# Moving one third of the score reading, the last rounding and two moment blocks in the last twelve steps of a fused attention kernel

## The reference, cut to what matters

```
L   = einsum('bhqd,bhkd->bhqk', q, k) * scale            # 16 heads, head_dim 8, causal
L_y = einsum('bhqd,bhkd->bhqk', q, k_y) * scale
agg = sum(exp(clip(L_y, -15, 15)) * mask, -1) + EPS
r   = log(abs(L) + EPS) - log(agg + EPS)
w   = softplus(r) * mask
A   = w / (sum(w, -1) + EPS)
x   = x + (A @ v, heads joined) @ w_proj.T
x   = x + 0.5 * ffn(layernorm(x))                        # needs mean and variance of every row
```

## Time and profile before

| what | value |
|---|---|
| median of 3 runs | 408.61 us (408.25 to 410.2) |
| the profiled execution's own time | 409.16 us |
| its span in the profile | 407.3 us |
| busy in the span: PE, DVE, ACT, POOL | 326.3, 295.5, 289.1, 209.0 us |
| mean granted clock of PE | 0.872 of full speed |
| the last twelve steps | from about 275.3 to 326.6 us of the span |

### The profile page before, as it was taken

One profiled execution on the slowest core, in us unless ns is written; L12 is line 12 of the kernel. 1 busy time (PEld: TensorE's weight loads), 2 busy tenths in 40 slices (PEclk: granted clock), 3 DMA queues, 4 the chain that ended last, 5 costly groups with the idle time before them and its releaser, 6 DMA issues.

```text
span 407.3 us, 8267 instructions
## 1 busy us (share of the span) xinstructions
PE 326.3 (80%) x2412; PEld 194.3 (48%) x2412; DVE 295.5 (73%) x628; ACT 289.1 (71%) x686; POOL 209.0 (51%) x348
## 2 busy tenths in 40 slices
PE   6879999995776545778877688788878998899992
PEld 6639999642243211213323223242334454499992
DVE  5664443288879988999998989989998747644431
ACT  2915556324989999999998989995667658255561
POOL 6575645300335475677776766784540014765542
PEclk9989999996589955868968958888999899899997
DMA  8786755134478989003000030000300086577640
GB/s 250 262 239 187 215 167 164 45 105 137 130 203 219 227 206 211 0 2 85 22 1 2 0 105 1 2 0 3 103 2 2 0 253 214 170 210 209 167 133 28
DMA packets 37993, 47.61 MB, mean 117 GB/s; under 512 B 4288, under 2 KB 26816, under 8 KB 37696
## 3 DMA queue, kind: packets, MB, share of 16 engines
q1 hardware_dynamic: 33616, 36.20, 33.1%
q0 software_dynamic: 2560, 6.30, 5.3%
q10 hardware_dynamic: 1776, 4.60, 3.4%
HBM read 24.02 MB, written 6.29 MB: 74 GB/s over the span
## 4 chain that ended last, share of the span: by engine, by line
PE 42%; DVE 21%; ACT 15%; issue 7%; DMA 6%; POOL 4%; SPq 2%; ACTq 1%; POOLq 0%; DVEq 0%
PE PS L1673 11%; PE PS L1683 10%; PE PS L1829 6%; DVE R L1412 6%; ACT R L1039 4%; ACT R L1029 4%; ACT CL L1029 4%; DVE CL L1397 3%; PE PS L1807 3%; PE PS L1607 3%; DVE agg L1421 2%; DMA R<-rows_d,R 2%; SPq L507 2%; ACT R L1049 2%; PE PS L1792 2%
## 5 line engine op out<-in xcount | busy, mean ns | idle before, releaser
L1412 DVE TENSOR_TENSOR R<-PS,MB 128x1024 int32<-128x1024 int32 (+1 forms) x76 | 84.6, 1132 | 12.3 <-PE PS L1807 11.7
L1039 ACT ACTIVATE R<-R 128x1024 f32<-128x1024 f32 x64 | 78.6, 1273 | 9.3 <-DVE R L1412 9.3
L916 ACT ACTIVATE R<-PS,R 128x128 f32<-128x128 f32 x184 | 52.6, 368 | 40.7 <-PE PS L1673 40.7
L1792 PE MATMUL PS<-R 64*128 64x512 bf16 (+3 forms) x256 | 40.2, 368 | 29.1 <-DVE CL L1397 15.7
L1829 PE MATMUL PS<-R,V 128*32 128x256 f32 (+3 forms) x512 | 56.0, 540 | 4.0 <-ACT R L1039 4.0
L1807 PE MATMUL PS<-QPS,R 64*128 64x512 bf16 (+3 forms) x256 | 38.0, 347 | 22.7 <-DVE CL L1397 18.1
L1673 PE MATMUL PS<-R 128*128 (+1 forms) x368 | 51.2, 282 | 1.4 <-DVE R L1278 0.9
L1683 PE MATMUL PS<-R 128*128 (+1 forms) x368 | 48.8, 276 | 0.7 <-ACT R L916 0.7
L1673 PEld LDWEIGHTS PS<-R 128*128 128x128 f32 x368 | 44.6, 191 | 4.2 <-issue 1.5
L1683 PEld LDWEIGHTS PS<-R 128*128 128x128 f32 x368 | 44.7, 192 | 1.1 <-ACT R L916 1.1
L1397 DVE SCALAR_TENSOR_TENSOR CL<-PS,MA 128x1024 f32<-128x1024 f32 x32 | 38.9, 1215 | 6.8 <-PE PS L1792 6.4
(11 more groups left out here) (189 smaller groups left out, 554.4 us busy)
## 6 DMA issues: line engine op xcount, KB each, us to landing
R<-w SPq DMA_DIRECT2D x38, 258.0 KB, 3.6
R<-R SPq DMA_DIRECT2D x32, 128.0 KB, 2.4
R<-R SPq DMA_DIRECT2D x16, 256.0 KB, 6.3
QPS<-R SPq DMA_DIRECT2D x32, 128.0 KB, 2.4
R<-w ACTq DMA_DIRECT2D x8, 258.0 KB, 4.3
rows_d<-X SPq DMA_DIRECT2D x8, 256.0 KB, 4.2
R<-w ACTq DMA_DIRECT2D x1, 2048.0 KB, 8.8
rows_d<-R SPq DMA_DIRECT2D x8, 256.0 KB, 2.5
```

The costliest lines, as they stand in the source:

```text
L916: last = act.activation(HT[:, k % 2, c * P:(c + 1) * P], PS[:, k % 2, c * P:(c + 1) * P], ACT.Gelu, bias=W1[:, k, F + c:F + c + 1])
L1039: act.activation(w, w, ACT.Ln, bias=1.0, scale=1.0).then_inc(s_ln, 1)
L1412: dve.tensor_tensor(weights(v)[:, :, at:at + n].bitcast(i32), PS[:, SLOTS[slot(b_fill(v, g))], 0:n].bitcast(i32), spread(mask, 1, 2), ALU. ...
L1792: last = pe.matmul(PS[:, SLOTS[slot(n)], :][:, par, at:at + (i + 1) * P], QS[rows, hp, (b * TB + i) * P:(b * TB + i + 1) * P], YS[rows, hp ...
```

## The change

It has five parts.

1. `by_act(v, g)` is now g == 2 for every unit. ACT reads group 2 in steps 32 to 43 too, and POOL clears the triangle of twelve more units. PE's piece 3 waits for that triangle.
2. The turned heads go back into `AV_BANK`, beside the weighed output, for all units. So piece 0 of the next pair waits for `heads_out` on DVE and no longer only for `av_out` on ACT.
3. The rounding of the last batch's q in step 33 moves from DVE to ACT (`scaled_q(3)`).
4. `moments` of batch 0 moves from step 25 to step 36, and of batch 1 from step 32 to step 38.
5. Some products that only keep PE busy go to another bank.

```diff
+MOMENTS_AT = (STEPS + 4, STEPS + 6)
+ROUNDED = (1, 2, 3)
 def by_act(v, g):
-    return v + LAG < STEPS and g == 2
+    return g == 2
...
             for s in range(END_STEP):
-                if 0 < s - LAG <= STEPS - LAG:
+                if 0 < s - LAG <= STEPS:
                     lower_triangle(s - LAG - 1)
...
                     if 0 <= v < STEPS:
                         logs(v, 0)
+                        magnitudes(v)
+                    if s == (NB - 1) * HP + Q_AT:
+                        scaled_q(NB - 1)
...
-                if b not in MIDDLE:
+                if b not in ROUNDED:
                     dve.wait_ge(s_qt, b + 1)
-                    if b:
-                        dve.wait_ge(s_qps, STACK_DMAS * b)
                     dve.tensor_copy(QP3[:, 0, :], PS[:, 7, :]).then_inc(s_qhi, 1)
...
                     if b and at == X_AT:
                         residual(b)
+                        if b >= len(MOMENTS_AT):
+                            moments(b)
+                    if b < len(MOMENTS_AT) and s == MOMENTS_AT[b]:
                         moments(b)
...
-                if j == 2 and by_act(v, 2):
+                if j == 2:
                     pe.wait_ge(s_low, v + 2)
-                if piece == 0 and v and ao_shared(v - 2):
-                    pe.wait_ge(s_aot, v // 2)
-                elif piece == 0 and v:
+                if piece == 0 and v:
                     pe.wait_ge(s_ao, v)
...
             def weighed_t(v):
                 pe.wait_ge(s_aot, v // 2 + 1)
-                if ao_shared(v):
-                    slot_free(ao_fill(v + 3))
...
-                    idle_products(6)
+                    idle_products(6, RANK_BANKS[1][0])
```

More of the change, by code:

```diff
@@ L163, in slot @@
     return n % 2 if n < 3 * TWO_SLOTS else (n + 2) % 3
[L166 to L181, removed]
 def build(nc, x_in, wattn_in, wg_in, w1_in, w2_in, b2_in, out):
@@ L1035, in logs @@
                 act.wait_ge(s_read, dve_reads(b_fill(v, (0, 2)[part])))
-                if part == 1 and by_act(v, 2):
+                if part == 1:
                     act.wait_ge(s_mag, v + 1)
@@ L1428, in heads_out @@
                 w = 2 * (HD + 1)
-                bank = ao_bank(v)
                 for par in range(2):
@@ L1433, in heads_out @@
                         AO.rearrange("p i h c -> p i (h c)")[:, :, at:at + w],
-                        PS[:, bank, AO_COL:AO_COL + TB * 2 * w].rearrange("p (i r) -> p i r", i=TB)
+                        PS[:, AV_BANK, AO_COL:AO_COL + TB * 2 * w].rearrange("p (i r) -> p i r", i=TB)
                         [:, :, par * w:(par + 1) * w]).then_inc(s_ao, 1)
@@ L1543, in between @@
                         den_reciprocal(b)
[L1544 to L1548, removed]
+                    if b == 0 and at == X_AT + 1 and g == 0:
+                        residual(b)
             for s in range(END_STEP):
@@ L1561, in _ @@
                 for g in range(3):
-                    if 0 <= v < STEPS:
+                    if 0 <= v < STEPS and not by_act(v, g):
                         abs_scores(v, g)
@@ L1781, in slot_free @@
                         pe.wait_ge(s_read, dve_reads(before))
-                    if n - 3 in HEADS_IN:
-                        pe.wait_ge(s_ao, HEADS_IN[n - 3])
             def scores_a(s, g):
@@ L1842, in weighed_t @@
                     at = AO_COL + i * 4 * (HD + 1)
-                    last = pe.matmul(PS[:, ao_bank(v), at:at + 4 * (HD + 1)],
+                    last = pe.matmul(PS[:, AV_BANK, at:at + 4 * (HD + 1)],
                                      AOT[:, i * P:(i + 1) * P], used, start=True, stop=True)
@@ L1977, in _ @@
                     pe.wait_ge(s_read, dve_reads(fills_before(END_STEP) - 1))
+                    pe.wait_ge(s_mag, STEPS)
                     gate(1, 0, 0, 2)
@@ L1980, in _ @@
                     gate(1, 0, 2, 8)
-                    idle_products(6)
+                    idle_products(6, RANK_BANKS[1][0])
                 if s == LN_EARLY + 1:
-                    idle_products(3)
+                    idle_products(3, RANK_BANKS[1][0])
                 if s == LN_EARLY + 2:
```

## The result

The changed kernel takes 411.54 us (median of 20 runs, 408.95 to 412.9) where the kernel before, timed beside it, takes 408.44 (20 runs, 405.6 to 410.2). The ratio is 1.0068, interval 1.0048 to 1.0088: 2.8 us more. The quotient of the two medians is 1.0076, 3.1 us. The forecast was +2.6 us, 411.2. The profiled execution took 411.08 us, with a span of 409.3.

The account below looks back on a forecast made before the run. It took DVE to set the pace before the change and ACT after it. Its terms, -1.9 rounding, +4.6 queue, -1.7 up to step 44 and +1.6 clock, gave +2.6 us: 411.2 against 408.61, range 406.5 to 413.5.

Parts of the forecast that it names:

- DVE loses 6.6 us net, step 25 gives nothing back: Last twelve steps: small reads and rounding leave DVE, moments come in, net 6.6 us less; step 25 set at 0.
- The rounding ends 1.9 us earlier: Step 33: the rounding of q, now on ACT, ends at 284.56 instead of 286.48, a gain of 1.9 us.
- The POOL queue: Step 35: piece 3 of pair 20 waits 4.8 us for a triangle behind 6.46 us of POOL work; +4.6 net.
- Steps 36 to 44 win 1.7 back, 1.0 of it because a low stretch doesn't recur: Steps 36 to 44: lateness falls from 2.7 to 1.0 us, with about 1.0 won by running at full clock.
- ACT becomes the bound: Last twelve steps: ACT needs 6.2 us for two steps, its loop through PE 6.8, against DVE's 6.0 before.
- The clock costs 1.6: PE's clock falls in or behind the wait of step 35, costing 1.6 us.
- the two clock terms: About 1.0 us gained from the low stretch before step 44 not recurring, 1.6 lost to a fall at the wait.
- The rival for that case: The POOL queue doesn't matter: -1.9 at step 36, -1.7 behind it, -3.6 in all, 405.0 us; chance 0.14.
- the rival of x11: Low stretches kept off the wait come elsewhere: ratio stays 1.007, mean clock as with twelve products; no chance given.

Follow-up runs that it names:

- x4: The kernel before with only the moments moved (batch 0 from step 25 to 36, batch 1 from 32 to 38): ratio 1.0012 to the kernel before.
- x2: The changed kernel with POOL's triangle of unit 21 put ahead of `query_part` of batch 3: 406.04 us, ratio 0.9954 to the kernel before.
- x6: The changed kernel with eight more small operations on POOL ahead of the series of batch 3: 414.86 us, ratio 1.0159 to the kernel before.
- x5: The kernel before with only the rounding of the last batch's q moved to ACT: ratio 1.0012 to the kernel before.
- x1: The changed kernel with `query_part` of batch 3 spread over steps 35 to 39 on POOL: 404.73 us, ratio 0.9949 to the kernel before.
- x3: The changed kernel with twelve unused products keeping PE busy before piece 3 of pair 20: 410.53 us, ratio 1.0072 to the kernel before.
- x11: The changed kernel with 18 unused products in the wait before piece 3 of pair 20: ratio 1.0053 to the kernel before.
- x8: x1 with the moments of batches 0 and 1 in steps 42 and 43 instead of 36 and 38: ratio 0.9953 to the kernel before.
- x7: x1 with rounding and moments back in their old places: ratio 0.9972 to the kernel before.

## Why the prediction was right

Step by step, in its own order:

- **DVE loses 6.6 us net, step 25 gives nothing back.** Right. Between the same two instructions DVE's busy time fell from 46.3 to 40.1 us, by 6.3. x4 shows the exchange in step 25: 1.24 us of waiting for 1.19 of moments.
- **The rounding ends 1.9 us earlier.** Right. From the scores of unit 21 the end comes at 5.98 us (282.15 + 0.60 - 276.77), before at 7.11 (285.80 + 0.68 - 279.37): 1.1 earlier. But the changed kernel was at the lower clock there. In x2 and x6, whose clock was full, it comes at 5.14 (283.56 + 0.60 - 279.02) and 5.13 (285.75 + 0.60 - 281.22), so 2.0 earlier than before. The forecast had 5.2 (284.56 - 279.4) and 1.9. DVE waited 0.86 for it here and 1.0 in those two, where about 1 was forecast. The wait for the DMAs into `QPS` at step 36 is gone, as predicted. Alone (x5) the term is worth nothing that can be measured. ACT's rows of the rounding in x2 and in x6:

```profile
283.56 0.60 ACT L1053 ACTIVATE R<-PS 128x512 bf16<-128x512 f32 x1
```

```profile
285.75 0.60 ACT L1053 ACTIVATE R<-PS 128x512 bf16<-128x512 f32 x1
```

- **The POOL queue.** Right in mechanism and in size, and shown by removing it (x1, x2) and by making it longer (x6). Terms and series: 6.46 forecast, 6.44 measured. Piece 3 of pair 20 was to come 12.9 us after the scores of unit 21 (279.4 to 292.3) and came at 13.7 (276.77 to 290.50). In x6, whose clock was full there, it came at 297.72 - 281.22 = 16.5, less the added 3.6: 12.9. The wait was to be 4.8. It was 3.43, because PE itself arrived late at the lower clock; in x6 it is 8.41 - 3.6 = 4.8. At full clock step 36 would so be 2.8 late, where 2.7 was forecast: 12.9 to piece 3 and 4.24 from there to piece 0 of pair 22 (x3) make 17.1, against 293.73 - 279.37 = 14.4 before. This is an estimate from rows of three traces. The other triangles are hidden, as predicted: PE waits for POOL only this once. There are ten of them beside those of units 21 and 22, not twelve.
- **Steps 36 to 44 win 1.7 back, 1.0 of it because a low stretch doesn't recur.** The 1.0 was a mistake. From piece 0 of pair 22 to piece 1 of pair 30 the changed kernel needs 32.3 us at full clock, against a forecast of 32.0 and against 33.6 before with its low stretch. In this one trace the term came true, but x1 (311.34, 1.94 us for a piece that takes 1.06), x2, x3 (314.33) and x11 have a low stretch again and need 33.3 to 33.4, while x6 and x8 have none and need 32.3 and 32.2. x5, which keeps the order of the kernel before in these steps, happens to have none either and needs 33.26. The stretch belongs to an execution, not to the kernel. At full clock on both sides these steps win 1.0 (33.26 to 32.30), where 0.7 was forecast apart from the stretch. The windows of the kernel before and of x5:

```profile
293.73:327.38 33.65, 28.72 (x262) 12.56 (x261) 28.58 (x47) 24.80 (x25) 4.71 (x10) 0.95 0.04 11
```

```profile
290.03:323.29 33.26, 27.27 (x263) 12.45 (x261) 29.04 (x48) 24.81 (x25) 4.76 (x10) 1.00 0.04 9
```

- **ACT becomes the bound.** Right. ACT is busy 28.9 of 32.3 us behind step 36 and DVE, now with gaps, 26.0; PE waits for its logarithms at the pieces 1 shown, and two steps take 7.07 us where 6.8 was worked out. In x8 easing DVE there gives nothing that can be measured.
- **The clock costs 1.6.** The fall came where it was forecast, inside the wait. Its local price is 2.6 in the changed kernel (6.85 against 4.24 us) and 1.6 in x6. But keeping the clock up there gave back nothing (x3) and 0.6 us (x11) by the ratios, about 1.0 by the medians. This term was probably too large, or is offset by low stretches elsewhere; by how much stays open, from nothing to about 2 us.

So the sum of +2.6 against a measured +2.8 is better than its parts, and part of that is luck. Two terms were off in opposite directions: 1.0 us booked as a gain that is not there, and 1.6 booked for the clock, of which little can be shown. Without these two the forecast was +2.0 (2.7 - 0.7), and the rows at full clock give +1.8 (2.8 - 1.0). That part was sound. Together the two clock terms were to add 0.6, and 1.0 is left for them in the measured +2.8. The part that decided the sign was right: without the order on POOL the same change is a gain. The rival for that case said 405.0, which is 3.6 us under the kernel before; x1 and x2 measured 0.9949 and 0.9954, 2.1 and 1.9 us under it (3.7 and 2.4 by the medians). Its 1.9 at step 36 holds: piece 0 of pair 22 comes 291.60 - 279.02 = 12.6 us after the scores of unit 21 in x2, 1.8 earlier than before. Its 1.7 behind that is the term with the 1.0 that is not there. The order was forecast to cost 411.2 - 405.0 = 6.2 us, and cost 4.9, with about 1.4 either way from the two intervals. The full-clock rows give 4.6 (12.9 of x6's distance against 287.33 - 279.02 = 8.3 in x2), which leaves about 0.3 for the clock at the middle. By the medians the order cost 6.8 (x1) or 5.5 (x2), which leaves more. The clock's share is thus as open here as in x3 and x11.

## What to carry to other kernels

When work is moved to an engine that has time to spare, its busy share says nothing of when the work is done: read what is written ahead of it in that engine's order, and who waits behind. Here one operation of 0.42 us behind 6.4 us of other work turned a gain of 0.5% into a loss of 0.7%, and the cure was to treat the last batch like the two before it. A low stretch of clock in one profile is no term to book as a gain, since it can turn up at another place in the next execution.

## What the hardware showed that I had not expected

With a wait of 3.4 us PE's clock was low for 6.8 us, 5.7 of them at work, and products put into the wait kept it at full, but the ratio hardly followed (1.0072 and 1.0053 against 1.0068). The traces suggest why, without showing it: where the low stretches of these steps fall differs from one profiled execution to the next. The two kernels whose clock fell in the wait, the changed one and x6, have no low stretch later in these steps. Those where it was kept up have one: x3 near 314, x11 near 305. x1 and x2, without the wait, have one near 311 and 300, but x7 and x8, without it too, have none. Over its runs the granted clock averages 0.874 in the changed kernel, 0.880 in x1 and in x11, and 0.876 in x3. The kernel before has 0.876 beside x1 and x3 and 0.877 beside x11. So by this measure twelve products bought back about a third of the difference to x1, and eighteen, on another chip, more of it, which the rival of x11 did not expect. The time still doesn't tell them apart. What decides where a stretch falls is open.
